# Reordering the late weighing, the turns and the residual step in a fused attention kernel

## What is computed

```python
a1 = _causal_attn(q1, k1, v1, scale, mask)
a2 = _causal_attn(q2, k2, v2, scale, mask)
y = jnp.concatenate([a1 - lp * a2, a1 + lp * a2], axis=-1)
x = _layernorm(x + y @ Wo.T)
# then three cycles of: out = out + coupling(out) * twist(out)
x = _layernorm(x + ffn(x))
```

## Time and profile before

| | us |
|---|---|
| median of 3 runs (lowest, highest) | 286.22 (285.04, 286.32) |
| the profiled execution, its own time | 286.54 |
| its span in the profile | 284.6 |
| PE busy | 250.5 (88%) |
| ACT busy | 220.8 (78%) |
| DVE busy | 203.1 (71%) |
| POOL busy | 86.3 (30%) |
| mean granted clock of PE | 0.964 of 2.4 GHz |

### The profile page before, as it was taken

One profiled execution on the slowest core, in us unless ns is written; L12 is line 12 of the kernel. 1 busy time (PEld: TensorE's weight loads), 2 busy tenths in 40 slices (PEclk: granted clock), 3 DMA queues, 4 the chain that ended last, 5 costly groups with the idle time before them and its releaser, 6 DMA issues.

```text
span 284.6 us, 9778 instructions
## 1 busy us (share of the span) xinstructions
PE 250.5 (88%) x3664; PEld 128.9 (45%) x3664; DVE 203.1 (71%) x752; ACT 220.8 (78%) x323; POOL 86.3 (30%) x241
## 2 busy tenths in 40 slices
PE   8259799999999999999999999989898899999990
PEld 4043444635546355463554635525363332222890
DVE  1778568687796877968779687771244478899993
ACT  3146789797897978979789797877976677888685
POOL 8740432425324253242532424321110000000373
PEclk9857999999999999999999999979999999999997
DMA  5302562553515516245252550644110164553045
GB/s 123 79 1 38 75 115 49 88 110 77 111 43 123 112 35 147 47 82 114 70 111 51 115 111 20 129 39 97 32 41 1 37 142 111 134 132 77 1 132 166
DMA packets 58217, 23.60 MB, mean 83 GB/s; under 512 B 42928, under 2 KB 56016, under 8 KB 58192
## 3 DMA queue, kind: packets, MB, share of 16 engines
q1 hardware_dynamic: 57904, 23.24, 38.6%
q10 hardware_dynamic: 288, 0.02, 0.1%
HBM read 5.04 MB, written 2.10 MB: 25 GB/s over the span
## 4 chain that ended last, share of the span: by engine, by line
PE 73%; ACT 12%; DVE 5%; issue 4%; DMA 2%; POOL 1%; ACTq 1%; DVEq 0%; POOLq 0%
PE O L614 11%; PE O L627 11%; PE S L746 7%; ACT probs_past L916 6%; PE S L512 5%; PE S L534 4%; PE M L660 3%; PE O L634 3%; PE M L646 3%; ACT o_sb L922 3%; PE S L545 3%; PE S L554 2%; DMA qk<-parts 2%; PE S L787 2%; PE M L671 2%
## 5 line engine op out<-in xcount | busy, mean ns | idle before, releaser
L916 ACT ACTIVATE probs_past<-S 128x1024 f32<-128x1024 f32 x64 | 64.6, 1039 | 12.9 <-PE S L502 12.9
L916 ACT ACTIVATE probs_late<-S 128x1024 f32<-128x1024 f32 x64 | 66.8, 1052 | 4.2 <-PE S L534 3.4
L614 PE MATMUL O<-probs_past,values 128*32 128x512 f32 x256 | 35.7, 629 | 11.9 <-ACT o_sb L922 11.3
L1160 DVE TENSOR_TENSOR roped<-rotated,rstd 128x128 f32<-128x128 f32 (+1 forms) x64 | 15.7, 302 | 17.9 <-POOL rstd L1531 17.9
L1516 POOL TENSOR_TENSOR minus_half_sum<-sum_eps,minus_half 128x40 f32<-128x40 f32 x16 | 4.5, 283 | 78.8 <-DVE estimate L1148 74.5
L627 PE MATMUL O<-probs_late,mixed 128*32 128x128 f32 x512 | 26.5, 279 | 0.1
L627 PE MATMUL O<-probs_late,values 128*32 128x128 f32 x512 | 25.7, 273 | 0.0
L1392 DVE SCALAR_TENSOR_TENSOR cY<-coup,ratio,Y 128x256 f32<-128x256 f32 x48 | 21.0, 480 | 5.8 <-ACT coup L999 5.0
L746 PE MATMUL S<-X,cn_w 128*128 128x512 f32 x48 | 25.0, 627 | 0.0
L1253 DVE RECIPROCAL rden<-M 128x64 f32<-128x64 f32 x15 | 8.4, 557 | 21.8 <-PE M L646 21.8
L512 PEld LDWEIGHTS S<-qk 32*128 32x128 bf16 x512 | 8.1, 93 | 30.8 <-issue 28.6
(11 more groups left out here) (187 smaller groups left out, 576.5 us busy)
## 6 DMA issues: line engine op xcount, KB each, us to landing
Y<-X SPq DMA_DIRECT2D x48, 128.0 KB, 2.4
xT_in<-in_xT SPq DMA_DIRECT2D x16, 128.0 KB, 2.7
x_res<-in_x SPq DMA_DIRECT2D x16, 128.0 KB, 2.1
out<-result SPq DMA_DIRECT2D x16, 128.0 KB, 1.9
future_in<-in_future SPq DMA_DIRECT2D x1, 256.0 KB, 3.1
qk<-parts SPq DMA_TRANSPOSE x15, 4.9
w_o<-in_w_o SPq DMA_DIRECT2D x2, 64.0 KB, 2.3
cn_w<-in_cn_w SPq DMA_DIRECT2D x2, 64.0 KB, 2.2
```

What stands on the lines that cost most here:

```text
L614: mm = pe.matmul(O[32 * g:32 * g + 32, :], values[p][:, 0, g, s, at:at + 32], probs_past[:, s, g, :], start=m == 0, stop=False)
L916: act.activation(dst, S[TILE_BUFFER[n]][:, :, :], ACT.Exp).then_inc(exp_done[n], 1)
L1160: last = dve.tensor_tensor(roped[:, at:at + n * G, :].rearrange("p (n g) d -> p g n d", g=G), rotated[:, t, lo * HD:hi * HD].rearrange("p ...
```

## The change

The nine tiles and all operations stay the same; the order within a step changes, on three engines.

On PE, steps 3 and 4 of the weighing of batch b - 1 are both done in step b, between the two past pairs; before, only step 4 was. `output_projection` of batch b - 2 comes directly ahead of them; before, that of batch b - 1 was the last thing in step b. `project` moves behind the second past pair. `turn_x1` moves behind `weigh(b, p, 1)`, `turn_outputs` ahead of the first half of the middle tile, and `weigh(b, p, 2)` and `turn_heads` ahead of its second half. After the last batch the remaining `output_projection`, `weigh` 3 and `weigh` 4 follow.

On ACT, `copy_projection` moves behind exponential 3 and `gate_tanh` ahead of exponential 6.

On DVE, `add_residual` is cut in two: the sum keeps the name, the row statistics become `output_moments`. The sum moves ahead of `normalize_queries`, the statistics stand between `normalize_queries` and `split`, and `sum_x1` moves from the end of the step to behind `normalize_heads`.

```diff
--- before.py
+++ after.py
@@ -675,33 +675,34 @@
                 first, second, last = (isinstance(b, int) and b == n for n in (0, 1, BATCH - 1))
                 project_more = not last and not (isinstance(b, int) and b == BATCH - 2)
                 past_pair(b, p, 0, general)
+                if not first and not second:
+                    output_projection(b - 2)
                 if not first:
+                    weigh(b - 1, 1 - p, 3)
                     weigh(b - 1, 1 - p, 4)
-                if project_more:
-                    project(b + 2, p, half_b + 1)
-                if first:
+                else:
+                    project(2, 0, 1)
                     if not general:
                         turn_queries(0, 0)
                     pe.wait_ge(n_["k_ready"], 2)
                 past_pair(b, p, 2, general)
+                if project_more and not first:
+                    project(b + 2, p, half_b + 1)
                 if first:
                     operands_turned(0)
                 weigh(b, p, 0)
                 late_pair(b, p, 4)
+                weigh(b, p, 1)
                 if not first and not second:
                     turn_x1(b - 2, project_more)
-                weigh(b, p, 1)
                 late_pair(b, p, 6)
-                middle_half(b, p, 8, 0)
                 if not first:
                     turn_outputs(b - 1, project_more)
-                middle_half(b, p, 8, 1)
+                middle_half(b, p, 8, 0)
                 weigh(b, p, 2)
                 if not first:
                     turn_heads(b - 1)
-                weigh(b, p, 3)
-                if not first:
-                    output_projection(b - 1)
+                middle_half(b, p, 8, 1)
                 if general and not last:
                     blocks_for_maximum(b + 1, 1 - p)
 
@@ -845,6 +846,8 @@
 
 
             last_b = BATCH - 1
+            output_projection(last_b - 1)
+            weigh(last_b, last_b % 2, 3)
             weigh(last_b, last_b % 2, 4)
             pe.wait_ge(n_["ffn_loaded"], 16 * FFN_LOADS)
             dense1(0, 0, True, 0, 1)
@@ -934,16 +937,16 @@
                 if not first:
                     copy_outputs(b - 1)
                 exponentials(b, 2)
+                exponentials(b, 3)
                 if project_more:
                     copy_projection(b + 2, p)
-                exponentials(b, 3)
                 exponentials(b, 4)
                 if not first and not second:
                     keep_x1(b - 2)
                 exponentials(b, 5)
-                exponentials(b, 6)
                 if project_more:
                     gate_tanh(b + 2, p)
+                exponentials(b, 6)
                 exponentials(b, 7)
                 if not first:
                     copy_heads(b - 1)
@@ -1265,6 +1268,8 @@
                 dve.wait_ge(res_loaded[p], (half_b + 1) * 16)
                 dve.tensor_tensor(summed[:, :, :].rearrange("p t d -> p (t d)"), bank[:, 0:T * 128],
                                   x_res[p][:, :, :].rearrange("p t d -> p (t d)"), ALU.add).then_inc(n_["summed_done"], 1)
+
+            def output_moments(b):
                 dve.wait_ge(n_["summed_done"], b + 1)
                 for t in range(T):
                     last = dve.bn_stats(stats[:, t, :], summed[:, t, :])
@@ -1296,21 +1301,20 @@
                     rotate(b + 2, p)
                 if not first:
                     normalize_heads(b - 1)
+                if not first and not second:
+                    sum_x1(b - 2)
                 if not last:
                     gate_values(b + 1, 1 - p)
-                if general:
-                    if not first:
-                        add_residual(b - 1, 1 - p, half_b - (1 - p))
-                    if not last:
+                    if general:
                         subtract_maximum(b + 1, 1 - p)
+                if not first:
+                    add_residual(b - 1, 1 - p, half_b - (1 - p))
                 if project_more:
                     normalize_queries(b + 2)
-                if not first and not general:
-                    add_residual(b - 1, 1 - p, half_b - (1 - p))
+                if not first:
+                    output_moments(b - 1)
                 if project_more:
                     split(b + 2)
-                if not first and not second:
-                    sum_x1(b - 2)
 
             def output_weights():
 
@@ -1440,6 +1444,7 @@
             normalize_heads(last_b, MB)
             sum_x1(last_b - 1)
             add_residual(last_b, 1, BATCH // 2 - 1, MA)
+            output_moments(last_b)
             normalize(last_b)
             sum_x1(last_b)
             steady_ratio(0)
```

## The result

The changed kernel takes 274.7 us in the median of four executions (273.47 to 275.09), against 285.63 before (284.78 to 286.32). The ratio is 0.961, with a 95% interval of 0.957 to 0.966: 3.9% faster. The forecast was 279.3 with a range of 275.5 to 283.5, so the direction was right and the gain was larger than the range allowed. The profiled execution took 273.47, its span in the profile is 271.3.

A forecast was written before the change was run, and what follows sets the result against it. PE was taken as nearest the bound, waiting 0.78 us per batch for ACT's copy of O. An end 8.3 us earlier and 1.4 for a clock fall gave -6.9 against the median 286.22: 279.3 us, range 275.5 to 283.5.

The forecast's parts named there:

- the waits of 1.10 and 0.82: DVE's waits per batch for POOL's root (1.10) and the turned outputs (0.82), left out of its own work of 9.6 us.
- the period of 11.25: Steady batches: 11.25 us each, taken from a loop of 11.09 to 11.40; ten batches make 178.8.
- The loop is 11.40, above PE's 11.03: Loop from output projection through DVE's sum to turn_heads and back: 11.40 us per batch, against PE's floor of 11.03.
- the choice between 11.09 and 11.40: Period with normalize_queries at 0.69 (POOL idle) or at 1.00 (mix_values beside it); 3 us apart over ten batches.
- The low price of normalize_queries: DVE's four normalize_queries instructions at 0.69 us with POOL idle, instead of 1.00 beside mix_values.
- Batches 2 and 3 at 12.0: Early batches whose transposing transfer lands after 6.2 us, so the next past pair starts at 12.0.
- One fall, 1.4: PE's clock falls once behind batch 1's transfer wait, where idle time grows from 0.90 to 1.9 or more; costs 1.4 us.
- The end part: What follows weigh 4 after the last batch: the same as before, x1 of batch 14 slightly earlier, counted at nothing.
- Rival 1: No clock fall, early transfers land in 4.9, PE and DVE meet at 11.09; about 274 to 277 us, chance 0.2.
- Rival 2: Part of PE's wait for o_sb stays, period 11.35 to 11.6; 283 us, chance 0.13.
- the 0.28: Time to spare at weigh 0: it could start at 3.55 us into the batch and PE reaches it at 3.83.
- Rival 4: Slower: the transposing transfer becomes the bound, period 12.4 if it lands after 6.6 every batch; 291 us, chance 0.07.

The follow-up runs named there:

- e1: PE's new order, with ACT and DVE left in their old order as in the kernel before; 279.68 us, ratio 0.979 to the kernel before.
- e11: The kernel before with DVE's new order alone; 285.19 us, ratio 1.000 to the kernel before.
- e10: The changed kernel with ACT's old order (copy_projection ahead of exponential 3, gate_tanh behind exponential 6); 277.13 us, ratio 0.971 to the kernel before.
- e15: The kernel before with ACT's new order alone; 288.04 us, ratio 1.010 to the kernel before.
- e12: The changed kernel with sum_x1 put back at the end of DVE's step; 278.06 us, ratio 0.974 to the kernel before.
- e5: The changed kernel with mix_values on POOL held back until the residual sum is done; 275.63 us, against 274.82 for the changed kernel beside it.
- e13: The changed kernel with twelve spare matmuls on PE at the end of batch 0; 273.04 us, ratio 0.957 to the kernel before.
- e8: The changed kernel run again without any edit, as a measure for the runs beside it; 274.82 us.
- e14: The changed kernel run again without any edit, as the measure beside the repeated spare-matmul run; 275.4 us.

## Why the prediction was right or wrong

**What bounded the kernel before: right, and incomplete.** The wait for ACT's copy of O set the batch, and its removal was foreseen as it came (copy at 2.84 against 2.85). What the forecast did not name is the second bound, 11.46, the loop of DVE and GpSimd alone, only 0.35 below 11.81. It read the waits of 1.10 and 0.82 as slack, but POOL's root and the wait for it are inside that loop. It did lay out DVE's new order, which opens the loop, so this cost no time in the sum. It is why PE's order alone gives 0.35 per batch (e1), DVE's alone nothing (e11), and both together 0.73 (e10). ACT's order brings the last 0.20; alone it costs 0.24 (e15). The forecast said of ACT's moves only that they change places inside its slack: that term, put at nothing, was worth 0.20 with the other two orders and cost 0.24 without them.

**The step that failed: the period of 11.25.** "The loop is 11.40, above PE's 11.03" and the choice between 11.09 and 11.40 made VectorE the bound. It is not: the loop through it is 10.67, and TensorE's own work, 10.88, sets the period. By terms: normalize_queries took 0.63 from start to start instead of 1.00; sum and statistics 0.34 + 0.80 instead of 1.28; split 2.25 for 2.30; normalize 0.57 for 0.52; rotate 2.96 for 3.03; reciprocal and heads 1.07 for 1.08; and until PE starts it is 0.06 for 0.2. The sum is 0.73 less, 10.67. The low price of normalize_queries would have given 11.09, still above PE. The other 0.42 is made of small things. The statistics had started 0.46 behind the sum, and now normalize_queries fills that (0.14). The handing over to PE was put too high (0.14). normalize_queries, split and rotate were taken with their last instruction in full, although the next one starts a little before it ends (0.06, 0.05 and 0.07). On PE the floor was read as 11.03 and came out at 10.88, 0.11 of it because weigh 3 now runs straight into weigh 4. Ten batches at 0.37 less are 3.7 us, most of the miss.

The rule that the prediction cites from the Trainium skill (SBUF — State Buffer, "Who interferes with whom"), that such a VectorE instruction contends with a GpSimd instruction that reads SBUF, pointed the right way. The runs agree with it: normalize_queries took 0.70 in the changed kernel with mix_values hardly beside it, 0.92 in e12, where they overlap in part, and 1.11 in e5, where mix_values runs wholly beside it.

**Batches 2 and 3 at 12.0: half right.** Batch 2 took 11.92, and PE waited 0.97 at its end for a transfer that landed after 6.6. Batch 3 took 10.89, as the transfer issued in it landed after 4.8. That is 1.1 us. In e13 PE waited 1.0 twice, so both batches were long there. Batch 14 took 11.75 for 11.3, its transfer landing after 6.4.

**The clock: the fall was right, its price low.** One fall, 1.4, was counted at batch 1. The profiled execution, after a gap of 3.02, had none and took 273.47; the other three took 274.49 to 275.09 at lower mean clocks (0.966 to 0.968 against 0.972), which fits a fall but has no rows to show it. Eight of the nine profiled executions that have PE's new order and no spare matmuls in the gap show the fall at batch 1. It cost 1.6 us in e8 and 2.7 in e14, and the spare matmuls take 1.8 and 2.4 us off the median. The price of 1.4 came from batch 14 of the kernel before, and there e11 confirms it: with the same wait of 1.06 and a granted clock of 1.00 its batch 14 took 11.80 and not 13.21.

**The end part: counted at nothing, brought 0.65.** From weigh 4 of the last batch to the end it took 271.30 - 198.17 = 73.13 against 284.60 - 210.82 = 73.78. PE had waited 0.43 there for x1 of batch 14 and does not now, because the output projection of that batch comes earlier. The other 0.2 was not traced.

The sum against the profiled execution: -6.9 forecast; -3.7 (period), -1.1 (batch 3), -1.4 (no fall in this one), -0.65 (end) and +0.45 (batch 14) give -13.3. The spans differ by 13.3 (284.6 to 271.3), the executions' own times by 13.1.

**The rivals.** Rival 1 came nearest, and its 274 to 277 holds the measured 274.7, but that is luck in part: the period is below its 11.09, while the clock did fall in most of the profiled executions, and one early transfer still landed after 6.6. Rival 2 did not occur, though the margin at weigh 0 was even thinner than the 0.28 said. With the old 0.70 from the copy's start, weigh 0 could have begun at 3.54, and it began at 3.69. Rival 4, the transfer as the bound, occurs in one or two batches of an execution, not in the steady ones.

## What to carry to other kernels

Before a wait is removed, add up every closed loop of engines, also those without the busiest one: here a loop of VectorE and GpSimd stood 3% behind the visible bound. TensorE's reorder alone brought 0.35 of the 0.93 us per batch, and those of VectorE and ScalarE without it nothing or less. A loop that is laid out on old distances and full durations comes out too long, because these hold small waits and overlaps that the new order fills; where it ends near another bound, give the range down to that bound. Where a reorder moves work from ahead of a long wait to behind it, look at what the clock does there, and fill the gap.

## What the runs showed of the hardware

The transposing transfers landed 4.8 to 4.9 us after they were issued in the steady batches, but 5.0 to 6.7 us after at batches 0 to 3 and 14 in single executions. In the changed kernel, from 47.5 to 55 us:

```profile
q8 instruction: 1, 0.02, 0.8%
q14 instruction: 1, 0.01, 0.7%
...
qk<-parts SPq DMA_TRANSPOSE x1, 6.6
```

In the windows of these slow ones there were transfers of instructions on other queues. In most of the steady windows looked at there were none, but two transfers that landed after 4.8 (changed kernel, from 59 us) and 4.9 (kernel before, from 176 us) had one as well. So this is a coincidence in time, and the cause wasn't tested.

The clock fell after gaps of 2.6 and 3.4 us (e14, e8) and not after one of 3.0 (the first profiled execution); in the kernel before it fell in batch 14 and not in batch 15 with the same wait of 1.06, and in e11 not in batch 14 either. The length of a gap alone doesn't decide it.
